# Forty normalizations of three layer norms given to GpSimd in a graph network kernel

## The reference

```
h = maximum(layernorm(x), 0)                  # stage 0
x = x + L0(h, edges, edge_weight)             # two aggregations over the edges
h = maximum(layernorm(x), 0)                  # stage 3
x = x + L1(h, edges, edge_attr)               # attention over 4 heads, segment softmax
h = maximum(layernorm(x), 0)                  # stage 4
x = x + L2(h, ...)                            # attention over 8 heads, q, k, v, output weights
h = maximum(layernorm(x), 0)                  # stage 6
x = x + L3(h, edges, Wt, Wg)                  # two gated aggregations
...
def layernorm(x, eps=1e-5): return (x - mean(x, -1)) / sqrt(var(x, -1) + eps)
```

## Time and profile before

| | us |
|---|---|
| median of 3 runs | 3535.09 |
| lowest and highest run | 3529.31 and 3539.81 |
| the profiled execution, its own time | 3526.88 |
| its span, first to last instruction | 3525.0 |
| busy PE / DVE / ACT / POOL | 2205.9 / 2399.7 / 1283.6 / 2004.9 |
| mean granted TensorE clock | 0.715 of full speed |

### The profile page before, as it was taken

The page is one execution under the profiler, slowest core; times in us unless marked ns, Lnnn a source line. Parts: engine busy times, 40 slices in busy tenths (PEclk is TensorE's granted clock), DMA queues, the critical chain, the costliest instruction groups (busy, mean ns, idle before and its releaser), DMA issues.

```text
span 3525.0 us, 60164 instructions
## 1 busy us (share of the span) xinstructions
PE 2205.9 (63%) x15246; PEld 1969.1 (56%) x15273; DVE 2399.7 (68%) x7660; ACT 1283.6 (36%) x3489; POOL 2004.9 (57%) x2076
## 2 busy tenths in 40 slices
PE   4992240566665567677556676545455455999998
PEld 3991230455554355555445575535455453998998
DVE  7997960777776669999726556575778777433434
ACT  4220020223332123333357767735777774000000
POOL 1777777777776477777267777716777770000000
PEclk9995555676666655555656556667777777999999
DMA  2210000111113123333333333224444441221222
GB/s 82 69 59 4 4 22 27 48 53 52 53 52 48 53 72 93 92 92 92 41 97 82 81 77 80 68 27 149 130 132 131 130 114 24 73 76 52 69 75 63
DMA packets 171637, 250.17 MB, mean 71 GB/s; under 512 B 52006, under 2 KB 120412, under 8 KB 171154
## 3 DMA queue, kind: packets, MB, share of 16 engines
q0 software_dynamic: 72704, 138.94, 16.2%
q1 hardware_dynamic: 94276, 96.20, 9.2%
q10 hardware_dynamic: 4430, 12.43, 1.0%
HBM read 217.00 MB, written 30.41 MB: 70 GB/s over the span
## 4 chain that ended last, share of the span: by engine, by line
POOL 48%; PE 21%; issue 18%; DVE 9%; DMA 2%; ACT 2%; DVEq 1%; POOLq 0%; ACTq 0%; SPq 0%
POOL arena L715 20%; POOL pool L715 17%; PE psum L1504 8%; POOL rec_dram L692 7%; PE psum L1500 5%; POOL ACC L715 3%; PE psum L1230 2%; DVE ACC L2336 1%; PE psum L1268 1%; DVE arena L2062 1%; ACT pool L816 1%; PE psum L1105 1%; DVE pool L2324 1%; DMA arena<-tab_dram,tblk 1%; DVE pool L1725 1%
## 5 line engine op out<-in xcount | busy, mean ns | idle before, releaser
L715 POOL DMA_INDIRECT arena<-tab_dram,tblk x832 | 796.6, 957 | 411.1 <-issue 250.8
L692 POOL DMA_INDIRECT rec_dram<-arena,ACC x400 | 396.1, 990 | 196.5 <-issue 118.9
L715 POOL DMA_INDIRECT pool<-tab_dram,arena x416 | 401.3, 965 | 131.4 <-issue 126.5
L1551 PE MATMUL psum<-pool 128*128 128x136 f32 (+1 forms) x1664 | 361.4, 398 | 82.8 <-DVE pool L2260 76.6
L1551 PEld LDWEIGHTS psum<-pool 128*128 128x128 f32 x1664 | 335.0, 289 | 94.9 <-issue 57.6
L1382 PE MATMUL psum<-pool 128*128 128x128 f32 x832 | 193.0, 426 | 294.6 <-DMA pool<-tab_dram,arena 206.9
L2116 DVE CAST pool<-pool 128x1024 f32<-128x1024 uint8 x264 | 182.4, 694 | 278.1 <-PE psum L1504 168.1
L2062 DVE TENSOR_SCALAR arena<-fwd,arena 128x128 bf16<-128x128 bf16 x2112 | 359.1, 287 | 0.8 <-PE psum L1424 0.8
L1382 PEld LDWEIGHTS psum<-pool 128*128 128x128 f32 x832 | 179.8, 328 | 299.0 <-DVE pool L2129 129.9
L715 POOL DMA_INDIRECT pool<-tab_dram,tblk x272 | 263.9, 970 | 125.5 <-issue 80.2
L857 ACT ACTIVATE arena<-psum,key 128x128 bf16<-128x128 f32 x416 | 146.4, 377 | 473.5 <-PE psum L1325 473.5
(11 more groups left out here) (373 smaller groups left out, 4891.7 us busy)
## 6 DMA issues: line engine op xcount, KB each, us to landing
pool<-items_dram SPq DMA_DIRECT2D x264, 128.0 KB, 2.1
pool<-dst_dram SPq DMA_DIRECT2D x104, 256.0 KB, 3.5
items_dram<-pool SPq DMA_DIRECT2D x132, 128.0 KB, 2.0
arena<-tab_dram,tblk POOLq DMA_INDIRECT x832
HN<-in_edge_attr_dram ACTq DMA_DIRECT2D x23, 500.0 KB
pool<-tab_dram,arena POOLq DMA_INDIRECT x416
rec_dram<-arena,ACC POOLq DMA_INDIRECT x400, 2.1
pool<-tab_dram,tblk POOLq DMA_INDIRECT x272
```

The costliest lines, as they stand in the source:

```text
L692: nc.gpsimd.indirect_dma_start(rec_dram, bass.IndirectOffsetOnAxis(ap=row_all[:, c:c + 1], axis=0), rec_all[:, c, :], None).then_inc(s_sca ...
L715: nc.gpsimd.indirect_dma_start(to[:, j, :], None, tab_dram[k], bass.IndirectOffsetOnAxis(ap=idx[:, G * g + j:G * g + j + 1], axis=0)).then ...
L1551: last_ = nc.tensor.matmul(bank[j // 3][:, (j % 3) * ww:(j % 3 + 1) * ww], OHF[:, half, j, :], weighed[k][:, half, j, :], start=True, stop ...
```

## The change

In stages 3, 4 and 6 DVE still takes the reciprocal of the first part, then increments `s_rooted` and normalizes none of its blocks. POOL has a new function `scale`, which waits for `s_rooted` and normalizes the 16, 8 and 16 blocks, incrementing `s_scaled` for each. It stands in POOL's queue ahead of pass 2's waits (stage 3), ahead of pass 3's (stage 4), and after the last gather (stage 6). PE waits for `s_scaled` for the chunks of the first part and for `s_normed` for the others. Stage 0 is as before. One semaphore at the start is merged into another.

```
--- before.py
+++ after.py
@@ -405,7 +405,6 @@
         s_placed = sem("s_placed")
         s_recbase = sem("s_recbase")
         s_recinit = sem("s_recinit")
-        s_recdef = sem("s_recdef")
         s_uemm = sem("s_uemm")
         s_ue = sem("s_ue")
         s_ea = [sem(f"s_ea{i}") for i in range(2)]
@@ -428,6 +427,8 @@
         s_wt = sem("s_wt")
         s_wtc = sem("s_wtc")
         s_normed = sem("s_normed")
+        s_scaled = sem("s_scaled")
+        s_rooted = sem("s_rooted")
         s_nodes = sem("s_nodes")
         s_divided = sem("s_divided")
         s_turned = sem("s_turned")
@@ -532,7 +533,9 @@
 
         T_CH = [(c, min(4, NB - 4 * c)) for c in range((NB + 3) // 4)]
         HALF = 4
-        LNS = {0: 0, 3: 1, 4: 2, 6: 3}
+        HALVES = {3: HALF, 4: 2, 6: HALF}
+        LNS = {0: 0, 3: NB, 4: 2 * NB - 4 * HALF, 6: 3 * NB - 4 * HALF - 8}
+        BY_POOL = {3: 0, 4: 4 * HALF, 6: 4 * HALF + 8}
         TURNED = {0: 0, 3: 1, 4: 2, 5: 3, 6: 4}
         SUMS = {1: 0, 2: 1, 7: 2}
         FLIPPED = (0, 1)
@@ -586,7 +589,7 @@
 
             for i in range(2):
                 sp.dma_start(ea[:, i, :], ea_v[:, i * 1024:(i + 1) * 1024]).then_inc(s_ea[i], 16)
-            sp.wait_ge(s_recdef, 1)
+            sp.wait_ge(s_recz, 2)
             sp.dma_start(rec_rows, recS[:, :, :].rearrange("p t r -> p (t r)")).then_inc(s_recinit, 16)
             sp.wait_ge(s_recinit, 16)
             sp.wait_ge(s_consts, 1)
@@ -677,7 +680,7 @@
             nc.gpsimd.memset(rec_all[:, :, :], 0.0).then_inc(s_recbase, 1)
             nc.gpsimd.memset(recS[:, :, :], 0.0).then_inc(s_recz, 1)
             pool.wait_ge(s_recz, 1)
-            nc.gpsimd.memset(recS[:, :, R_DST], float(P)).then_inc(s_recdef, 1)
+            nc.gpsimd.memset(recS[:, :, R_DST], float(P)).then_inc(s_recz, 1)
             nc.gpsimd.memset(resets[:, :, 1:RUN], 1.0).then_inc(s_resets, 1)
             nc.gpsimd.memset(resets[:, :, 0], 0.0).then_inc(s_resets, 1)
 
@@ -692,7 +695,15 @@
                     nc.gpsimd.indirect_dma_start(
                         rec_dram, bass.IndirectOffsetOnAxis(ap=row_all[:, c:c + 1], axis=0),
                         rec_all[:, c, :], None).then_inc(s_scat[g % 3], 16)
+            def scale(stage):
+
+                pool.wait_ge(s_rooted, list(HALVES).index(stage) + 1)
+                for b in range(4 * HALVES[stage]):
+                    nc.gpsimd.tensor_scalar(HN[:, b, :], X[:, b, :], meanvar[:, b, 0:1], stat[:, 4, b:b + 1], ALU.subtract, ALU.mult).then_inc(s_scaled, 1)
+
             for k in range(4):
+                if k >= 2:
+                    scale(k + 1)
                 pool.wait_ge(s_stored[k], 16 * CHUNKS)
                 pool.wait_ge(s_idx, 1 if k == 0 else 3)
                 idx = idx_u if k == 0 else idx_s
@@ -715,6 +726,7 @@
                         nc.gpsimd.indirect_dma_start(
                             to[:, j, :], None, tab_dram[k],
                             bass.IndirectOffsetOnAxis(ap=idx[:, G * g + j:G * g + j + 1], axis=0)).then_inc(landed, 16)
+            scale(6)
 
 
         @block.scalar
@@ -1080,7 +1092,10 @@
                 def work(c, n):
                     g = before(stage, c, TURNED)
                     if stage in LNS:
-                        pe.wait_ge(s_normed, NB * LNS[stage] + 4 * c + n)
+                        if c < HALVES.get(stage, 0):
+                            pe.wait_ge(s_scaled, BY_POOL[stage] + 4 * c + n)
+                        else:
+                            pe.wait_ge(s_normed, LNS[stage] + 4 * (c - HALVES.get(stage, 0)) + n)
                     else:
                         pe.wait_ge(s_divided, c + 1)
                     if g >= 2:
@@ -1836,7 +1851,7 @@
 
             ft3 = FT[:, :].rearrange("p (b f) -> p b f", b=NB)
 
-            def norm_stats(c, n, half=HALF):
+            def norm_stats(c, n, half=HALF, by_pool=False):
 
                 for b in range(4 * c, 4 * c + n):
                     queued(v.bn_stats(lnst[:, b, :], X[:, b, :]))
@@ -1848,7 +1863,7 @@
                 elif c + 1 == CHUNKS:
                     norm_ask(4 * half, NB)
                 if c == half:
-                    norm_answer(0, 4 * half)
+                    norm_answer(0, 4 * half, by_pool)
                 elif c + 1 == CHUNKS:
                     norm_answer(4 * half, NB)
 
@@ -1859,11 +1874,13 @@
                 dve.sem_inc(s_sq_in, 1)
                 asked[0] += 1
 
-            def norm_answer(lo, hi):
+            def norm_answer(lo, hi, by_pool=False):
 
                 dve.wait_ge(s_sq_out, asked[0])
                 link(v.reciprocal(stat[:, 4, lo:hi], stat[:, 3, lo:hi]))
-                for b in range(lo, hi):
+                if by_pool:
+                    dve.sem_inc(s_rooted, 1)
+                for b in range(lo, lo if by_pool else hi):
                     v.tensor_scalar(HN[:, b, :], X[:, b, :], meanvar[:, b, 0:1], stat[:, 4, b:b + 1], ALU.subtract, ALU.mult).then_inc(s_normed, 1)
 
             def chunk_of(t, c, n):
@@ -1881,7 +1898,7 @@
                     of = turned_back(stage, c, n)
                     v.tensor_tensor(chunk_of(X, c, n), chunk_of(X, c, n), of, ALU.add).then_inc(s_taken, 1)
                     dve.wait_ge(s_taken, before(stage, c, MADE) + 1)
-                    norm_stats(c, n)
+                    norm_stats(c, n, HALF, True)
                 return work
 
             def feature_chunk(t, c, n):
@@ -2519,7 +2536,7 @@
             def add_divided(c, n):
                 link(divided(c, n))
                 link(v.tensor_tensor(chunk_of(X, c, n), chunk_of(X, c, n), chunk_of(HN, c, n), ALU.add))
-                norm_stats(c, n, 2)
+                norm_stats(c, n, 2, True)
 
             flow((0, add_divided))
             for c, n in T_CH:
```

3 lines of the change are left out of this document (1 added, 2 removed).

## The result

The changed kernel takes 3548.1 us (median of 5 runs, 3547.33 to 3549.96) where the kernel before takes 3534.78 (5 runs, 3529.31 to 3539.81): ratio 1.0042, 95% interval 1.0027 to 1.0057, 13.3 us between the medians. The forecast was no change, 3534.6 us, and its range ended at 3545.

The account below looks back on a forecast made before the run. POOL's gathers, waiting on table stores, carry 48% of the chain. Stage 3 -0.22, stage 6 -0.73 and stage 4 +1.45 sum to 0.5 us faster: 3534.6 us, no change, range 3527 to 3545.

Parts of the forecast that it names:

- Passes unchanged in length: Sign expected in the changed profile: the passes with POOL's gathers keep their length.
- Price on POOL: Each normalization moved to POOL takes 0.40 us, between an IOTA's 0.225 and a gather's 1.26; DVE's price is 0.257.
- PE takes the chunks in order, so POOL's lateness at chunk 1 is what costs: Stages 3 and 6: PE needs blocks 4 to 7 for turn(1), so block 8's lateness loses 1.24 us in each.
- The two stalls that go: PE's wait for DVE's table copy in stage 3 (1.02 us won) and for ACT in stage 6 (0.51 us won).
- Stage 4: Before pass 3, DVE-bound: DVE moves on 2.05 us sooner, less 0.60 for contention with POOL, net 1.45 us won.
- The port: Stage 4: about three two-input DVE instructions may wait for POOL, bounds 0 and 1.2 us, taken as 0.60.
- The rival in which DVE waits for all eight: Stage 4: DVE's first two-input instruction waits 3.2 us for all eight POOL instructions; in all 2.1 us slower, 3537.2; chance 0.13.
- A pause of POOL ahead of arithmetic: Rival: POOL pauses 2.86 us before arithmetic after gathers, delaying stages 3 and 6 in full; 3540.3 us; chance 0.04.
- The clock: PE's low granted clock, 0.74 and 0.68 of full speed in stages 3 and 6; PE's shifts were reckoned from old durations.
- a price of 0.6 to 0.95 (0 to 10 us slower): Rival: each POOL normalization costs 0.6 to 0.95 us, making the kernel 0 to 10 us slower; chance 0.05.
- The rival for slower by over 0.3%: POOL too slow: at the gather's 1.26 us per normalization 22.7 us slower, 3557.8; passes 0.3% from about 0.95; chance 0.06.
- a pass that changes its own length: Listed sign of being wrong: passes that change their own length, which nothing in the prediction foresees.

Follow-up runs that it names:

- split kernel: Changed kernel, but in stages 3 and 6 DVE normalizes chunks 0 and 1, POOL chunks 2 and 3, product behind stages 3 and 4: 3529.52 us, ratio 0.999.
- h_all_product: Changed kernel plus one POOL product of 128x1 that nothing reads behind the normalizations of stages 3 and 4: 3540.34 us, ratio 1.0023 to before.
- e_only4: Kernel before with POOL normalizing in stage 4 alone: 3535.36 us, ratio 1.0013 to before.

## Why the prediction was wrong

- **"Passes unchanged in length"**: this is the step that failed and that brought the time past 0.3%. I priced what POOL's new instructions delay and put what they leave behind at nothing. The gathers behind them were 10 ns longer, 832 times: passes 2 and 3 took 8.2 us more, where the three stages together lost 4.8. It hits the 48% of the chain that I had read as fixed. Fast gathers again, in h_all_product, gave 8.4 us back. The runs show that it goes with the arithmetic instruction that stands last ahead of the gathers; what in POOL, or in the program as built, does it they do not show.
- **Price on POOL**: 0.40 forecast, 0.786 measured, nearly double, and three times DVE's 0.257 (the 0.51 that stands beside my price was too low as well). I fitted a rate from a MEMSET and an IOTA, 2.42 ns an element and 0.11 us besides; with reading it is 3.33 and 0.37. With 0.786 in my own formulas, stage 3 loses 8 x 0.529 + 0.10 - 1.02 = 3.3 (measured 3.0), stage 6 4.33 - 0.51 = 3.8 (measured 3.5). This term was mis-sized and its mechanism right: it is why the stages lose 4.8 us where the sum had them win 0.5. By itself it would have stayed within 0.3%.
- **PE takes the chunks in order, so POOL's lateness at chunk 1 is what costs**: right. The split kernel, which takes only that away, turns both losses into gains.
- **The two stalls that go**: right. From turn(3) to turn(4) of stage 3 it is 2.63 us in the changed kernel (1771.41 to 1774.04) instead of 3.60, and in stage 6 PE has no wait for ACT's copy.
- **Stage 4**: 1.45 forecast, 1.70 measured. At 0.96 us per normalization PE had barely the room: its first product, from 2379.11, takes 3.62 us, and chunk 2 follows at 2382.52 without the 6.87 us of waiting that it had before.
- **The port**: I took 0.60 us for three DVE instructions, half a POOL instruction each. DVE's instructions with two SBUF inputs were lengthened by 0.03 to 0.14 us, 0.35 in all. POOL gives more: of its eight normalizations of stage 4 those beside DVE's took 0.86 to 1.30 us, the others 0.79, so the mean is 0.96 (7.67 / 8). The rival in which DVE waits for all eight is wrong. The Trainium skill ("SBUF — State Buffer", section "Who interferes with whom") says that a VectorE instruction with two SBUF inputs contends with a GpSimd one that reads SBUF; it calls the shared ports an exclusive lock and says, of VectorE's two-port modes, that the loser waits for the whole instruction. The trace agrees that there is contention. A wait as long as a whole instruction, 0.7 to 0.8 us, it does not show: the largest is 0.51.
- **A pause of POOL ahead of arithmetic**: wrong. POOL starts within 0.2 us of DVE's signal, and its first normalization takes 0.80 us in stages 3 and 6, as the others do. The first of stage 4 is the 1302 ns of the line below, beside two instructions of DVE.
- **The clock**: I moved PE's work later at unchanged speed. In three of five profiles with POOL's blocks first in stage 3 that was wrong by 4 to 5 us (35.4 to 36.2 us instead of 31.3). In the other two, the first among them, the clock rose as long after PE got chunk 1 as before, 3 to 4 us.

```profile
L702 POOL TENSOR_SCALAR HN<-X,stat x40: 782/792/1302, 1758.8 to 3008.2; 128x128 f32<-128x128 f32 x40
```

Of the rivals, "a price of 0.6 to 0.95 (0 to 10 us slower)", to which I gave 0.05, is what the stages did. The rival for slower by over 0.3% needed a price of 0.95; that came out by another mechanism, which none of my rivals had, though I had named a pass that changes its own length among the signs of being wrong.

## What to carry to other kernels

Before moving work to an idle engine, count the instructions that this engine executes afterwards on the critical path, and compare their least durations before and after: 10 ns on 832 gathers outweighed three stages. Such a difference costs only where that engine paces the pass. Give the slow engine the blocks that its consumer needs last, not the first part. And where PE starts from a low clock, look at when it rises: here it rose 4 to 10 us after the start with the chunks at once, and 10 or 18 us after it with the chunks one by one.

## What the runs showed of the hardware

- After TENSOR_SCALAR on POOL, with operands from SBUF or constants, its indirect DMAs took 10 to 11 ns longer each (940 to 951, 942 to 952 ns at least), through one or two whole passes. A TENSOR_TENSOR behind it, of 384 elements or of one (0.19 us), undid it; a MEMSET of one element did not. Why is open: nothing here looks into POOL.
- In the kernels whose later gathers were slow, the fastest gathers of passes 0 and 1, ahead of any normalization, were at 942 to 944 ns instead of 938 to 940, 4 ns more than in the other kernels of the same chip. No TENSOR_SCALAR had run on POOL by then, so this part goes with the program as a whole and not with what ran last; of the 10 to 11 ns some 7 to 10 then come as a step between passes of one kernel (942 to 952 between passes 2 and 3 of e_only4). This too is open.
- On POOL a product of two tensors of 128x384 (1.006 us) is cheaper than a TENSOR_SCALAR of the same size with two operands from SBUF (1.648 us).
- On POOL a TENSOR_SCALAR of 128x128 beside DVE instructions with two SBUF inputs took 0.86 to 1.30 us instead of 0.79 (stage 4 of the changed kernel).
- With the increment of the semaphore for POOL, DVE stands idle 0.15 us ahead of its next instruction (the bracket in the split kernel's first row), where it was 0.03 before.
